# Second attention: an unread 128-row matmul ahead of each natural score pair

## The chip, the cores and the metric

One Trainium2 chip, one NeuronCore of it. The metric is the device time of one execution in microseconds, the median of several runs. TensorE's clock is granted by the chip at one of two levels, 2.4 GHz (shown as 1.00 or 9 in the profile) and 1.2 GHz (0.50 or 5).

## What is computed

Two blocks, each a gated attention and a gated feed-forward part on 2048 tokens of width 128. The part that matters here is the attention of the second block, after a layer norm. x has the shape (1, 2048, 128), so all 2048 tokens attend to each other, in 16 heads of width 8:

```python
qkv = (jnp.einsum('bnd,ed->bne', x, qkv_w) + qkv_b).reshape(b, n, H, 3 * HD)
q, k, v = jnp.split(qkv, 3, axis=-1)
attn = jax.nn.softmax(jnp.einsum('bhqd,bhkd->bhqk', q, k) * SCALE, axis=-1)
out = jnp.einsum('bhqk,bhkd->bhqd', attn, v)
out = out.transpose(0, 2, 1, 3).reshape(b, n, d)
return jnp.einsum('bnd,ed->bne', out, fc_w) + fc_b + x
```

In front of it stand a spectral attention with convolutions and a three-layer feed-forward part; behind it a mixture of eight experts of which two are chosen for each token.

## The kernel before, in words

Each engine runs a program of its own, written out by hand in order, with semaphores between them. The second attention is the part of TensorE's program between L738 and the end of the steps.

Layout. The 16 heads are four head groups (hg) of four heads (g). A head has 8 dimensions, and its queries and keys are stacked so that they take 32 rows of the array: head g of a group lies in rows 32g to 32g+31 of `Ks` and `Qb` (single-pass fp32r). Four matmuls that use the four different strips can run side by side.

Two kinds of scores are computed. *Natural* scores (`nat`, L768) have queries on the output partitions; VectorE takes their maximum per query (L1215). A natural item k has four matmuls of 32 rows by 512 columns into PSUM banks 0 to 3, as two pairs: pair 0 is heads 0 and 1, pair 1 is heads 2 and 3. Each pair waits until VectorE has reduced what the two banks held (`nat_max`, L765) and signals `nat_ready`. *Transposed* scores (`scores(g)`, L828) have keys on the output partitions, and take the negated maximum in as two more rows of `Qb`; they go to three rotating banks (4, 5, 7), ScalarE takes the exponential (L484), and `values` (L806) multiplies by V into bank 6: 128 rows by 16 columns, one column strip for each head, in two passes, eight records.

Order. A query block qb has 512 queries and there are four; a step s is one head group and one block of 128 keys (kt = s % 16), so 64 steps a query block, 256 in all, in groups of 16. The natural items run 20 steps ahead (`LEAD`). A step on TensorE is

```python
scores(0); nat(qb, s - 1 + LEAD, 1); scores(1); values(qb, s - 1)
scores(2); nat(qb, s + LEAD, 0); scores(3)
```

with the transposes of the maxima (`max_rows`, L780) after it in step kt = 13 and those of the finished outputs (`turn_outputs`, L794) in step kt = 2. A group's first step waits for the maxima to be in `Qb` (`mrow_in`): VectorE copies them (L1241), and SyncE writes them with eight transfers (L277). Steps 4 to 67 of a query block are a hardware loop run three times; the first four steps and the last sixty are written out. Natural items end 20 steps before the last step.

Ahead of the steps stands an opening loop of 16 natural items (32 pairs) between the projections (`stack`, L742: 128 rows by 512 columns, two-pass fp32) and the value tiles (L751), and then four natural items by themselves. Behind the steps come the output projection and the experts (`three`, L676 to L678: 128 rows by 512 columns in single-pass fp32r; `down`, L935; a transpose of 8 rows, L955).

Of the kernel before, what the change touches and what calls it, by code (L numbers as in the profile page):

```python
# [19 lines left out]
P = 128  # L20
# [49 lines left out]
def adaln_pair(nc, x_in, consts_in, mods_in, spectral_in, ffn_in, attn_in, moe_in, out):  # L70
    with ExitStack() as ctx:
        def sb(name, shape, dt=F32, where=ctx):
            return where.enter_context(nc.sbuf_tensor(name, shape, dt))
# [78 lines left out]
        with l1:  # L152
            Ks = sb("Ks", [P, HG, TOK], F32R, where=l1)
# [49 lines left out]
        def bank(n):  # L203
            return ps[:, n, :]
# [8 lines left out]
        def due(count):  # L213

            return not isinstance(count, int) or count > 0
# [29 lines left out]
        def between(slot):  # L245

            total = len(stacks) - early + NT // 2
            lo, hi_ = early + total * slot // 32, early + total * (slot + 1) // 32
            n = len(stacks)
            return range(min(lo, n), min(hi_, n)), range(max(lo, n) - n, max(hi_, n) - n)  # L250
# [305 lines left out]
        def _(pe):  # L556
# [3 lines left out]
            for layer in range(2):  # L560
                for k in range(6):
                    last = pe.matmul(ps[:, 7, 6 * layer + k:6 * layer + k + 1],
                                     dw_[f"wmod{layer}"][:, k * P:k * P + P], silu[:, layer:layer + 1],
                                     start=True, stop=True)
            last.then_inc(sem.mod_ready, 1)

            for u in range(8):
# [3 lines left out]
                for i in range(2):  # L571
                    last = pe.matmul(ps[:, u % 4, i * 4 * M:(i + 1) * 4 * M], z[:, 2 * u + i, :], dw_["dft"],
                                     start=True, stop=True)
# [6 lines left out]
            for n in range(4):  # L580
                for i in range(2):
                    b = 2 * n + i
                    last = pe.matmul(ps[:, 4 + n, 256 * i:256 * i + 256], sw["qw"][:, b * P:b * P + P], low_flat,
                                     start=True, stop=True)
                last.then_inc(sem.qkv_ready, 1)
            for j in range(2):
                last = pe.matmul(ps[:, 0, 256 * j:256 * j + 256], sw["kw"][:, j * P:j * P + P], low_flat,
                                 start=True, stop=True)
            last.then_inc(sem.qkv_ready, 1)
            for ri in range(2):  # L590
                last = pe.matmul(ps[:, 1, 256 * ri:256 * ri + 256], low_flat[:, ri * P:ri * P + P], sw["vw"],
                                 start=True, stop=True)
# [24 lines left out]
            for i, (ri, j) in enumerate(groups):  # L617
# [6 lines left out]
                if i + 4 < len(groups):  # L624
# [4 lines left out]
                          start=True, stop=True).then_inc(sem.o_ready, 1)  # L629
# [6 lines left out]
            for ri in range(2):  # L636
                pe.wait_ge(sem.gelu_ready, ri + 1)
                for half in range(2):
# [3 lines left out]
                              start=True, stop=True).then_inc(sem.pw_ready, 1)  # L642
# [8 lines left out]
            for b in range(4):  # L651
                pe.wait_ge(sem.yT_copied, b + 1)
                pe.matmul(bank((5 + b) % 8), dw_["idft"], YT[:, 4 * b:4 * b + 4, :].rearrange("p t d -> p (t d)"),
                          start=True, stop=True).then_inc(sem.idft_ready, 1)
# [83 lines left out]
            def stack(n):  # L738
                kq, hg, tb = stacks[n]
                if due(n - 3):  # L740
                    pe.wait_ge(sem.kq_done, n - 3)
                pe.matmul(bank(4 + n % 4), aw[("kw1", "qw1")[kq]][:, hg * P:hg * P + P],  # L742
                          hT[:, tb * 512:tb * 512 + 512], start=True, stop=True).then_inc(sem.kq_ready, 1)

            def value_tiles(u):
                pe.wait_ge(sem.kq_done, min(len(stacks), len(stacks) - 3 + u))
                if due(u - 3):
                    pe.wait_ge(sem.v_copied, u - 3)
                for i in range(2):
                    t = 2 * u + i  # L750
                    last = pe.matmul(ps[:, 4 + u % 4, 256 * i:256 * i + 256], hT[:, t * P:t * P + P], aw["vw1"],  # L751
                                     start=True, stop=True)
                last.then_inc(sem.v_ready, 1)

            def nat(qb, k, pair):

                hg, qt, c = k // 16 % 4, k % 16 // 4, k % 4
                item = 64 * qb + k
                if pair == 0 and k % 16 == 0:
                    if isinstance(qb, int) and qb == 0 and k == 0:  # L760
                        pe.wait_ge(sem.first_filled, 1)
                    else:
                        pe.wait_ge(sem.q_filled, 4 * qb + k // 16)
                if due(2 * item + pair - 1):
                    pe.wait_ge(sem.nat_max, 2 * item + pair - 1)  # L765
                for g in (2 * pair, 2 * pair + 1):
                    rows = slice(32 * g, 32 * g + 32)
                    last = pe.matmul(bank(g), Qb[rows, hg, qt * P:qt * P + P], Ks[rows, hg, c * 512:c * 512 + 512],  # L768
                                     start=True, stop=True)
                last.then_inc(sem.nat_ready, 1)  # L770
# [39 lines left out]
            def step(qb, s):  # L810
# [21 lines left out]
                if not first and not (last_block and s - 1 + LEAD >= 64):  # L832
                    nat(qb, s - 1 + LEAD, 1)
# [4 lines left out]
                if not (last_block and s + LEAD >= 64):  # L838
                    nat(qb, s + LEAD, 0)
# [8 lines left out]
            pe.wait_ge(sem.kq_done, early)  # L848
            for k in range(16):
                for half in range(2):  # L850
                    nat(0, k, half)
                    some_stacks, some_values = between(2 * k + half)
                    for n in some_stacks:
                        stack(n)
                    for u in some_values:
                        value_tiles(u)
# [621 lines left out]
```

## Time and profile before

| | us |
|---|---|
| Median of 3 runs | 1482.05 |
| Lowest, highest | 1471.12, 1508.8 |
| The profiled execution, its own time | 1492.91 |
| Span of its profile (first to last instruction) | 1491.1 |
| Mean granted TensorE clock in it | 0.842 |

PE is the matmul side of TensorE, PEld its weight loads, DVE VectorE, ACT ScalarE, POOL GpSimd, SPq the queue of SyncE. L828 is line 828 of the kernel. Matmul records overlap and their ends are modelled, so starts are the sounder thing to compare. Times in the profile's views are microseconds from the start of the span.

### The profile page before, as it was taken

Reading aid. Unit: us, or ns where it says so; the run is one execution under the profiler, and the core shown is the slowest. Engines: PE = TensorE matmul, PEld = TensorE weight load, DVE = VectorE, ACT = ScalarE, POOL = GpSimd, SP = SyncE. Lnnn points to the kernel's source line nnn. Section 1 sums busy time; section 2 is a strip of 40 time slices with the busy share of each in tenths; the row PEclk is TensorE's granted clock in tenths of the full one; section 3 lists DMA queues with packets and bytes.
Section 4 is the critical chain, followed back from the end, with each engine's and each line's share of the span. In section 5 each row is a group of like instructions: output and inputs, shape, how many; then the busy total and the mean of one; then the engine's idle time right before and its main releaser. Section 6 shows DMA issues by size and latency. Waiting matters only on the chain.

```text
span 1491.1 us, 19855 instructions
## 1 busy us (share of the span) xinstructions
PE 1271.4 (85%) x6846; PEld 620.4 (42%) x6846; DVE 874.1 (59%) x1244; ACT 796.4 (53%) x1423; POOL 18.0 (1%) x25
## 2 busy tenths in 40 slices
PE   4767999887988888888879988988898869999998
PEld 4435787332232222223322222322222127787877
DVE  4756442797687786778866578777870052122122
ACT  3335442433576676667755567666775554344442
POOL 0010000000000000000000000000000000000000
PEclk9868999795598897889975579878985579999999
DMA  8000000000000000000000000000000000000000
GB/s 330 1 1 0 0 0 1 0 0 1 1 1 2 1 2 3 1 2 1 1 3 1 1 1 2 1 2 1 2 1 1 0 0 1 7 1 7 0 7 7
DMA packets 9279, 14.82 MB, mean 10 GB/s; under 512 B 4320, under 2 KB 8544, under 8 KB 8672
## 3 DMA queue, kind: packets, MB, share of 16 engines
q1 hardware_dynamic: 8896, 10.84, 2.0%
q10 hardware_dynamic: 288, 2.76, 0.4%
q8 instruction: 53, 0.87, 0.2%
q14 instruction: 42, 0.34, 0.1%
HBM read 12.29 MB, written 1.05 MB: 9 GB/s over the span
## 4 chain that ended last, share of the span: by engine, by line
PE 65%; DVE 13%; ACT 11%; SPq 4%; issue 4%; DMA 2%; DVEq 0%; ACTq 0%
PE ps L806 19%; PE ps L828 17%; PE ps L935 8%; ACT probs L484 7%; DVE mx L1215 5%; PE ps L676 5%; PE ps L678 4%; PE ps L677 4%; SPq L277 4%; DMA Qb<-mT 2%; ACT eh L536 1%; PE ps L713 1%; PE ps L916 1%; PE ps L742 1%; PE ps L794 1%
## 5 line engine op out<-in xcount | busy, mean ns | idle before, releaser
L1215 DVE TENSOR_REDUCE mx<-ps 128x2 f32<-128x1024 f32 x512 | 605.6, 1218 | 183.0 <-PE ps L768 179.7
L484 ACT ACTIVATE probs<-ps 128x512 f32<-128x512 f32 x1024 | 534.3, 599 | 321.3 <-PE ps L828 319.7
L828 PE MATMUL ps<-Qb,Ks 32*128 32x512 f32 x1024 | 368.4, 574 | 111.8 <-ACT probs L484 71.9
L828 PEld LDWEIGHTS ps<-Qb,Ks 32*128 32x128 f32 x1024 | 145.9, 219 | 510.4 <-ACT probs L484 347.3
L806 PE MATMUL ps<-probs,V 128*16 128x512 f32 x2048 | 353.3, 756 | 0.0
L768 PE MATMUL ps<-Ks,Qb 32*128 32x512 f32 x1024 | 260.5, 561 | 14.3 <-DVE mx L1215 8.4
L536 ACT ACTIVATE eh<-ps,MW 128x512 f32<-128x512 f32 x128 | 87.9, 688 | 95.3 <-PE ps L678 94.6
L768 PEld LDWEIGHTS ps<-Ks,Qb 32*128 32x128 f32 x1024 | 105.7, 216 | 53.3 <-DVE mx L1215 35.2
L935 PEld LDWEIGHTS ps<-MW,eh 128*128 128x128 f32 x1024 | 118.3, 192 | 2.6
L935 PE MATMUL ps<-MW,eh 128*128 128x128 f32 x1024 | 119.2, 275 | 0.0
L1358 DVE SCALAR_TENSOR_TENSOR acc<-ps,gate,acc 128x128 f32<-128x128 f32 x128 | 36.0, 344 | 129.3 <-PE ps L935 128.8
L806 PEld LDWEIGHTS ps<-probs,V 128*16 128x16 f32 x2048 | 40.8, 98 | 80.2 <-ACT probs L484 52.5
L676 PE MATMUL ps<-hT,ew 128*128 (+1 forms) x128 | 56.7, 443 | 2.8
L678 PE MATMUL ps<-hT,ew 128*128 (+1 forms) x128 | 50.4, 394 | 0.0
L677 PE MATMUL ps<-hT,ew 128*128 (+1 forms) x128 | 50.3, 393 | 0.0
L1248 DVE RECIPROCAL rden<-ps 128x16 f32<-128x16 f32 x16 | 4.0, 248 | 76.5 <-PE ps L794 76.5
L1170 DVE TENSOR_TENSOR act_b<-bf,act_b 128x512 fp32r<-128x512 f32 x16 | 11.1, 692 | 58.9 <-ACT bf L435 58.9
L742 PE MATMUL ps<-hT,AW 128*128 128x512 f32 x64 | 38.9, 709 | 0.9 <-ACT hT L337 0.9
L676 PEld LDWEIGHTS ps<-hT,ew 128*128 128x128 f32 x128 | 24.0, 188 | 26.6 <-ACT eh L536 21.5
L676 PE MATMUL ps<-act_a,h 128*128 128x512 f32 x64 | 25.2, 394 | 1.6 <-DVE act_a L1147 1.6
L678 PEld LDWEIGHTS ps<-hT,ew 128*128 128x128 f32 x128 | 24.1, 188 | 5.7
L666 PE MATMUL ps<-CW,z 128*128 128x128 f32 x48 | 12.4, 430 | 16.4 <-DVE z L987 16.4
(214 smaller groups left out, 1026.9 us busy)
## 6 DMA issues: line engine op xcount, KB each, us to landing
MW<-moe_in SPq DMA_DIRECT2D x1, 4454.0 KB, 23.8
FW<-ffn_in SPq DMA_DIRECT2D x1, 2824.5 KB, 12.4
Qb<-mT SPq DMA_DIRECT2D x128, 2.0 KB, 1.7
SW<-spectral_in ACTq DMA_DIRECT2D x1, 1479.5 KB, 9.6
DW<-mods_in ACTq DMA_DIRECT2D x1, 1219.0 KB, 6.2
x<-x_in SPq DMA_DIRECT2D x4, 256.0 KB, 10.7
out<-x SPq DMA_DIRECT2D x4, 256.0 KB, 2.3
AW<-attn_in SPq DMA_DIRECT2D x1, 836.5 KB, 13.9
```

The lines of the kernel that those rows point to most:

```text
L277: sp.dma_start(Qb[row:row + 1, hg, :].bitcast(F32), mT[4 * part + g:4 * part + g + 1, :].bitcast(F32)) \
L484: act.activation(probs[:, 4 * (s % 2) + g, :], bank(score_bank[4 * (s % 16) + g]), ACT.Exp, scale=SCALE1) \
L536: act.activation(eh[:, e % 2, fb, :], bank(fb % 2), ACT.Relu, bias=mw["eb1"][:, col:col + 1]).then_inc(sem.eh_copied, 1)
L676: pe.matmul(to, w[0], v[0], start=start, stop=False)
L677: pe.matmul(to, w[0], v[1], start=False, stop=False)
L678: return pe.matmul(to, w[1], v[0], start=False, stop=stop)
L742: pe.matmul(bank(4 + n % 4), aw[("kw1", "qw1")[kq]][:, hg * P:hg * P + P], hT[:, tb * 512:tb * 512 + 512], start=True, stop=True).then_inc ...
L768: last = pe.matmul(bank(g), Qb[rows, hg, qt * P:qt * P + P], Ks[rows, hg, c * 512:c * 512 + 512], start=True, stop=True)
L806: last = pe.matmul(ps[32 * g:32 * g + VW, 6, :], V[:, kt, col:col + VW], probs[:, 4 * (s % 2) + g, :], start=(kt == 0), stop=(kt == 15))
L828: pe.matmul(bank(score_bank[n]), Ks[rows, hg, kt * P:kt * P + P], Qb[rows, hg, :], start=True, stop=True).then_inc(sem.st_ready, 1)
L935: last = pe.matmul(ps[:, 2 + e % 2, qt * P:qt * P + P], eh[:, e % 2, fb, qt * P:qt * P + P], mw["ew2"][:, col:col + P], start=(fb == 0), s ...
L1215: dve.tensor_reduce(mx[:, k // 16 % 2, k % 16 // 4, k % 4, 2 * pair:2 * pair + 2], ps[:, 2 * pair:2 * pair + 2, :], AX, ALU.max) \
```

## The change

`nat` gets a parameter, true except in the opening loop of 16 items. Where it is true, a matmul of 128 rows by 512 columns in fp32r (weights: the first 128 columns of the head group's `Ks`; moving: the 512 columns of the pair's keys) is issued into the first bank of the pair, after the pair's wait and ahead of its two matmuls. It starts and stops its own accumulation, and the pair's first matmul overwrites the bank.

```diff
-            def nat(qb, k, pair):
+            def nat(qb, k, pair, filled=True):
...
                 if due(2 * item + pair - 1):
                     pe.wait_ge(sem.nat_max, 2 * item + pair - 1)
+                if filled:
+                    pe.matmul(bank(2 * pair), Ks[:, hg, 0:P], Ks[:, hg, c * 512:c * 512 + 512], start=True, stop=True)
                 for g in (2 * pair, 2 * pair + 1):
...
             for k in range(16):
                 for half in range(2):
-                    nat(0, k, half)
+                    nat(0, k, half, False)
```

## Rows read from the trace of the kernel before

**Rows 1.** The page: busy time of each engine, and TensorE's granted clock in 40 slices

```profile
PE 1271.4 (85%) x6846; PEld 620.4 (42%) x6846; DVE 874.1 (59%) x1244; ACT 796.4 (53%) x1423; POOL 18.0 (1%) x25
...
PEclk9868999795598897889975579878985579999999
```

**Rows 2.** Stretches: length; PE, PEld, DVE, ACT, POOL busy (count); clock, DMA share, GB/s

```profile
349.40:408.60 59.20, 54.80 (x234) 14.18 (x237) 35.77 (x34) 30.18 (x58) 0.00 (x0) 0.50 0.00 1
408.60:459.80 51.20, 41.66 (x296) 14.57 (x292) 43.89 (x43) 37.91 (x73) 1.23 (x2) 1.00 0.01 2
770.40:862.60 92.20, 84.32 (x363) 21.47 (x363) 53.17 (x51) 45.85 (x88) 0.61 (x1) 0.50 0.01 1
...
1122.00:1200.50 78.50, 65.53 (x232) 14.65 (x232) 1.23 (x3) 39.59 (x77) 0.00 (x0) 0.50 0.00 1
```

**Rows 3.** Timeline, full clock: start, duration, engine, line, [idle before <-releaser]

```profile
696.13 0.72 PE L828 MATMUL ps<-Qb,Ks 32*128 32x512 f32 x2
...
696.65 2.06 ACT L484 ACTIVATE probs<-ps 128x512 f32<-128x512 f32 x4 [0.57 <-PE ps L828]
...
697.30 0.50 PE L828 MATMUL ps<-Qb,Ks 32*128 32x512 f32 x1 [0.33 <-ACT probs L484]
...
697.73 1.09 PE L806 MATMUL ps<-probs,V 128*16 128x512 f32 x8
...
698.76 0.72 PE L828 MATMUL ps<-Qb,Ks 32*128 32x512 f32 x2
```

**Rows 4.** Timeline, a step at half clock

```profile
841.23 0.79 PE L828 MATMUL ps<-Qb,Ks 32*128 32x512 f32 x1
...
841.83 0.62 PE L828 MATMUL ps<-Qb,Ks 32*128 32x512 f32 x1
...
842.71 0.79 PE L828 MATMUL ps<-Qb,Ks 32*128 32x512 f32 x1 [0.25 <-ACT probs L484]
...
843.43 1.91 PE L806 MATMUL ps<-probs,V 128*16 128x512 f32 x8
845.26 0.28 PEld L828 LDWEIGHTS ps<-Qb,Ks 32*128 32x128 f32 x1 [1.69 <-issue]
```

**Rows 5.** Timeline, opening loop at full clock: natural pair, projection, natural pair

```profile
286.11 0.50 PE L768 MATMUL ps<-Ks,Qb 32*128 32x512 f32 x2
...
286.54 0.30 PEld L742 LDWEIGHTS ps<-hT,AW 128*128 128x128 f32 x2 [0.25 <-issue]
...
287.60 0.18 PEld L768 LDWEIGHTS ps<-Ks,Qb 32*128 32x128 f32 x2 [0.76 <-issue]
```

**Rows 6.** Timeline, experts: 128-row matmuls in a row, both clocks; then 8 rows

```profile
1258.28 0.40 PE L677 MATMUL ps<-hT,ew 128*128 128x512 f32 x1
1258.51 0.40 PE L678 MATMUL ps<-hT,ew 128*128 128x512 f32 x1
...
1230.83 0.63 PE L678 MATMUL ps<-hT,rw 128*128 128x512 f32 x1
1231.26 0.63 PE L676 MATMUL ps<-hT,rw 128*128 128x512 f32 x1
...
1252.96 0.39 PE L678 MATMUL ps<-hT,ew 128*128 128x512 f32 x1
1253.28 0.96 PEld L955 LDWEIGHTS ps<-MW,gtT 8*128 8x128 f32 x8 [0.35 <-issue]
```

**Rows 7.** Timeline: transposes of outputs (half clock) and maxima, and a group's first score

```profile
833.41 1.11 PE L794 MATMUL ps<-CW,U 128*128 128x128 f32 x4
...
834.45 0.79 PE L828 MATMUL ps<-Qb,Ks 32*128 32x512 f32 x1
...
652.41 0.60 PE L780 MATMUL ps<-CW,m 128*8 128x128 f32 x4 [0.58 <-ACT probs L484]
...
652.94 0.49 PE L828 MATMUL ps<-Qb,Ks 32*128 32x512 f32 x1
...
660.42 0.49 PE L828 MATMUL ps<-Qb,Ks 32*128 32x512 f32 x1 [2.94 <-DMA Qb<-mT]
```

## The prediction

> **What bounds the kernel now.** I read the page first. TensorE is busy for 85% of the span, the other engines for at most 59%, and the row of the granted clock is uneven between the tenth and the thirty-third of the forty slices, which is the second attention [rows 1]. So the second view is the table of stretches, cut where the clock changes [rows 2]. At full clock (1.00, which is 2.4 GHz) the stretch 408.6 to 459.8 us runs 73 exponentials, that is 18.3 steps at four per step, or 2.80 us a step with all group ends in it. At half clock (0.50, 1.2 GHz) the stretch 770.4 to 862.6 runs 88, that is 22 steps at 4.19 us. The attention ends at 1200.5, and of its 850 us the half clock holds 59, 92 and 78 us in three long stretches [rows 2], the rest in short dips. In both states TensorE's records cover over 80% of the stretch.
>
> The third view is the timeline of single steps. At full clock [rows 3] a step repeats every 2.63 us (696.13 to 698.76): a cluster of scores and natural pairs, whose small matmuls use different 32-row strips and run side by side; 0.52 us after its start the first of four exponentials begins; the score at 697.30 waits 0.33 us for an exponential to free its bank; the values of the step before start at 697.73, when the last exponential that they need is done, and take 1.02 us. TensorE is the longest part of that loop but has a gap in it. At half clock [rows 4] the same loop takes 4.03 us (841.23 to 845.27); values take 1.84 us of it.
>
> **The change, part by part.** It adds to each natural pair, except the 32 of the opening loop, one 128-row weight load and one matmul of 512 columns. Natural pairs number 512 (two for each of 256 items), so 480 fillers: 8 before the steps, 472 in steps 0 to 236 of 256. The last 20 steps have no natural pairs and get none. No wait is added: the wait on the row maximum, already there, now stands ahead of the filler. No transfer, no VectorE, ScalarE or GpSimd work is added. Nobody reads the filler, but TensorE takes its matmuls in order, so everything behind it is later.
>
> What does one cost? The trace has it in two forms. Between matmuls of its own kind (128 rows, 512 columns, single pass) starts are 0.23 us apart at full clock and 0.43 at half, the next weights loading underneath [rows 6]. But the filler stands between 32-row matmuls. Where the trace changes the rows used, the next weight load doesn't start until the matmul ahead has run out: from a natural pair at 286.11 to the load of a 128-row matmul at 286.54 are 0.43 us [rows 5], and from a 128-row matmul at 1252.96 to an 8-row load at 1253.28 are 0.32 us without a load of its own [rows 6]; with the load, about 0.11 more, that is again 0.43. From the 128-row matmul the natural pair follows only after it has run out too, at 287.60 [rows 5]. At half clock the same block is 0.72 us (score at 842.71 to values at 843.43 [rows 4]). Bounds for a filler: 0.23 to 0.43 us at full, 0.43 to 0.72 at half. Below nothing is possible only through the clock, and is treated with the rivals. I take the upper ends, because they are the rows with a change of rows in them, in both directions.
>
> The filler also cuts the clusters. The order of a step is score 2, filler, natural pair 0, score 3, score 0 of the next step, filler, natural pair 1, score 1, values. Score 2 now stands alone: one block. Natural pair 0 with score 3 is a block, and score 0 shares rows with the pair, so it follows as a second wave: at full clock that costs 0.22 more (0.72 against 0.50 us for one [rows 3]), at half 0.43 more (841.83 + 0.62 against 841.23 + 0.79 [rows 4]). Natural pair 1 with score 1 is one block. A step is then:
> full clock: 4 x 0.43 (score 2, two fillers, pair 1 with score 1) + 0.65 + values 1.02 = 3.39 us, against 2.63;
> half clock: 4 x 0.72 + 1.15 + 1.84 = 5.87 us, against 4.03.
> The gaps in which TensorE waited for exponentials (0.33 us at full clock) are used up in this; four exponentials (2.06 us [rows 3]) and two maxima fit inside either step, so neither ScalarE nor VectorE is late next. TensorE has no gap left.
>
> **Which clock.** This decides. Before the steps the clock is at half from 340, with VectorE setting the pace of the natural pairs; fillers fill part of those gaps but leave others, so I expect the steps to begin at half clock as now. Does the filler lift it? In the old half-clock step the columns stream, weighted by the share of the array's rows in use, for 1.71 us in the values (four passes at 0.43 [rows 6]) and 0.43 x (1 + 0.75 + 0.25) in the scores and pairs: 2.56 of 4.03 us, 64%. In the new one it is 1.71 + 0.43 x (0.25 + 1 + 0.75 + 0.25 + 1 + 0.75) = 3.42 of 5.87 us, 58%. So a step gets no denser: running out and reloading eat what the filler adds. The old, denser step stayed at 0.50 from 349.4 to 408.6 and from 770.4 to 862.6 [rows 2]. So I take it that the new one stays at half clock through the filled steps. At full clock the share is 1.71 of 3.39, 50%, beside 1.28 of 2.63, 49%, which held; the full clock would hold too, once reached.
>
> The Trainium skill, "TensorE: Matmul & The Clock Gate", section "Why this matters for your kernels", says the opposite: keep TensorE continuously busy and it comes to the full clock. By that rule the filled steps run at 3.39 us and the time is that of the second rival. The trace doesn't bear it out: TensorE's records cover 84.32 of 92.2 us at 0.50 [rows 2].
>
> **The sum.** Steps start at 352 (349.4 now [rows 2], and some 2.6 for eight fillers). 236 filled steps x 5.87 = 1385. In 14 groups the output transposes (833.41 to 834.45, 1.04 us at half) and the maximum transposes (652.41 to 652.94, 0.53 at full [rows 7], say 0.8 at half) also cut the second wave off its first, 0.29 each: 14 x 2.42 = 34. The stall at a group's start goes: from the maximum transposes at 652.41 to the score at 660.42 that waits for the transfers are 8.0 us [rows 7], and two steps of 5.87 cover that. Last 20 steps at half clock as now: 78.5 us for 77 exponentials [rows 2], 4.08 a step, 82. End of the attention 1853. The tail is unchanged: 1491.1 - 1200.5 = 290.6, and 1.8 lies outside the span (1492.9 less 1491.1). 1853 + 290.6 + 1.8 = 2145 us. The profiled execution is 11 us above the median of the runs shown; where the clock is pinned that luck falls away, so I correct nothing. If the clock does this, 2090 to 2180.
>
> **Rivals.**
> Late escape: the half clock is left somewhere and kept for a part. For it: at 862.6 the old kernel got out of a long stretch with no change of pattern [rows 2], and the shares above are near each other. Against it: 58% is under 64%. Halfway between this forecast and the next rival, 1850.
> Full clock from the first steps: 352 + 236 x 3.39 (800) + 14 x 1.95 (27: transposes 0.6 and 0.53, 0.22 for each cut, and 0.4 of stall, since two steps of 3.39 cover nearly all of the 8.0) + 82 + 290.6 + 1.8 = 1553. Against it: the steps start at half clock, see above. Still slower.
> Not slower: the fillers' loads hide under the matmul ahead. Mechanism: the pitch of 0.23 us [rows 6] holds in the clusters too; two fillers then add 0.46 us where 0.33 to 0.6 of gap is; a full-clock step stays near 2.7 us, and at half clock the share that streams rises to 3.42 in about 4.6 us, 74%, so that the clock comes up soon. 352 + 236 x 2.7 (637) + 14 x 5 for group ends + 82 + 292 = 1433. It decides as soon as a filler costs under about 0.3 us at full clock. Against it stand the 0.43 us of [rows 5]; for it, that the 128-row matmul there is a two-pass one.
> The Trainium skill, same page, section "Part 2: What happens when you issue a matmul", has this rule: a weight load is pulled ahead of running matmuls when it goes to the background weight buffer. By it the time is this rival's; the 0.23 us pitch agrees, the 0.43 us across a change of rows doesn't.
>
> **Numbers.** Half clock throughout 0.50, late escape 0.22, full clock 0.14, hidden 0.12, the rest for what I don't see. The range 1540 to 2180 takes in the first three. A measurement of this kernel tells about 2% from no change: 1452 to 1512. The hidden case lies two thirds under that and one third in it. Faster 0.08, same 0.05, slower 0.87.
>
> **What would show it.** Right: a line of its own with 480 matmuls; a filler's load 0.4 us (full) or 0.7 us (half) behind the score ahead; steps of 5.9 or 3.4 us with no idle ahead of L828 from ScalarE; ScalarE waiting longer for scores; granted clock 0.50 from 350 to about 1850; no transfer wait at group starts. Wrong: filler loads starting within 0.15 us of the matmul ahead, or a clock row at full height in the attention.

## The result, and the profile after

The changed kernel takes 2165.62 us (median of 4 runs, 2160.24 to 2168.71); the kernel before, run beside it, 1495.42 (1471.12 to 1512.06). The ratio is 1.466, 95% interval 1.456 to 1.477. Ratios are of the fast runs of each kernel alone; in the experiments below that leaves out two of the four runs of the kernel with strips, one of which took 1860 us.

The page of the changed kernel: the engines, TensorE's granted clock in 40 slices, and two of the costliest groups (busy us, mean ns | idle before, and what ended it). The filler is L767, the natural matmuls L770, the scores L830, the values L808.

```profile
PE 2043.8 (95%) x7326; PEld 852.4 (39%) x7326; DVE 896.0 (42%) x1244; ACT 846.4 (39%) x1423; POOL 18.0 (1%) x25
...
PEclk9789995555555555555555555555555555699999
...
L484 ACT ACTIVATE probs<-ps 128x512 f32<-128x512 f32 x1024 | 584.3, 596 | 935.4 <-PE ps L830 934.0
...
L767 PE MATMUL ps<-Ks 128*128 128x512 f32 x480 | 381.7, 795 | 2.3 <-DVE V L1211 2.2
```

The clock row that was uneven [rows 1] is now flat at half through the whole second attention. 480 fillers are there. ScalarE does the same 1024 exponentials and now waits 934 us for scores: TensorE has become the bound of every filled step. The stretches show the same (length, busy time of PE, PEld, DVE, ACT, POOL, clock): the filled steps, the last twenty, the tail.

```profile
343.99:1781.72 1437.73, 1427.44 (x4353) 441.15 (x4352) 603.13 (x570) 550.14 (x957) 7.36 (x12) 0.50 0.00 1
1781.72:1868.60 86.88, 72.80 (x265) 16.65 (x262) 4.47 (x9) 44.06 (x84) 0.00 (x0) 0.51 0.00 1
1868.60:2158.40 289.80, 268.27 (x1636) 211.19 (x1634) 79.68 (x261) 122.11 (x184) 0.00 (x0) 0.98 0.01 4
```

TensorE's records cover 1427 of 1438 us, and the clock is 0.50 all along. The 290.6 us behind the attention are 289.8 now, so all of the loss lies in it: 851 us (349.4 to 1200.5 [rows 2]) have become 1525.

The timeline of one filled step, beside [rows 4]:

```profile
899.97 0.79 PE L770 MATMUL ps<-Ks,Qb 32*128 32x512 f32 x2
...
901.12 0.80 PE L767 MATMUL ps<-Ks 128*128 128x512 f32 x1
...
901.84 0.28 PEld L770 LDWEIGHTS ps<-Ks,Qb 32*128 32x128 f32 x2 [0.44 <-issue]
...
902.57 1.91 PE L808 MATMUL ps<-probs,V 128*16 128x512 f32 x8
...
904.41 0.28 PEld L830 LDWEIGHTS ps<-Qb,Ks 32*128 32x128 f32 x1 [1.69 <-issue]
...
905.13 0.80 PE L767 MATMUL ps<-Ks 128*128 128x512 f32 x1
...
905.86 0.79 PE L770 MATMUL ps<-Ks,Qb 32*128 32x512 f32 x2
```

From 899.97 to 905.86 are 5.89 us. Read the starts: two waves of pair 0, score 3 and score 0 take 1.15, the filler 0.72, pair 1 with score 1 0.73, the values 1.84, score 2 alone 0.72, and the second filler 0.73 before pair 0 again. The weight loads wait 0.44 us with "issue" as the cause: nothing that the profile shows holds them. I read these waits as the matmul ahead running out of the array; the runs below bear on that.

### The profile page after: what moved, and what is told of

It reads as the page before. It is cut to its first block, busy times and chain, and to the rows that moved or that the text cites. A ratio compares the mean times of both kernels' runs of the same rounds, so it can differ in the third digit from the quotient of the medians.

```text
span 2158.4 us, 20815 instructions
## 1 busy us (share of the span) xinstructions
PE 2043.8 (95%) x7326; PEld 852.4 (39%) x7326; DVE 896.0 (42%) x1244; ACT 846.4 (39%) x1423; POOL 18.0 (1%) x25
## 4 chain that ended last, share of the span: by engine, by line
PE 90%; DVE 5%; ACT 3%; issue 1%; DMA 1%; SPq 0%; DVEq 0%; ACTq 0%
PE ps L808 22%; PE ps L770 16%; PE ps L767 16%; PE ps L830 15%; PE ps L937 5%; PE ps L676 3%; PE ps L678 3%; PE ps L677 3%; DVE mx L1217 1%; ACT eh L536 1%; ACT probs L484 1%; PE ps L796 1%; PE ps L782 1%; PE ps L713 1%; PE ps L918 1%; PE ps L742 1%
## 5 line engine op out<-in xcount | busy, mean ns | idle before, releaser
L1217 DVE TENSOR_REDUCE mx<-ps 128x2 f32<-128x1024 f32 x512 | 627.2, 1225 | 834.2 <-PE ps L770 834.0
L484 ACT ACTIVATE probs<-ps 128x512 f32<-128x512 f32 x1024 | 584.3, 596 | 935.4 <-PE ps L830 934.0
L830 PE MATMUL ps<-Qb,Ks 32*128 32x512 f32 x1024 | 706.2, 759 | 22.9 <-ACT probs L484 22.9
L808 PE MATMUL ps<-probs,V 128*16 128x512 f32 x2048 | 489.1, 1048 | 0.0
L830 PEld LDWEIGHTS ps<-Qb,Ks 32*128 32x128 f32 x1024 | 264.3, 292 | 481.2 <-issue 427.5
L770 PE MATMUL ps<-Ks,Qb 32*128 32x512 f32 x1024 | 396.2, 772 | 7.8 <-DVE mx L1217 5.2
L767 PE MATMUL ps<-Ks 128*128 128x512 f32 x480 | 381.7, 795 | 2.3 <-DVE V L1211 2.2
L770 PEld LDWEIGHTS ps<-Ks,Qb 32*128 32x128 f32 x1024 | 142.6, 276 | 242.8 <-issue 215.7
L767 PEld LDWEIGHTS ps<-Ks 128*128 128x128 f32 x480 | 138.2, 288 | 253.2 <-issue 229.6
L808 PEld LDWEIGHTS ps<-probs,V 128*16 128x16 f32 x2048 | 38.1, 107 | 113.0 <-issue 105.5
L676 PEld LDWEIGHTS ps<-hT,ew 128*128 128x128 f32 x128 | 24.0, 188 | 26.6 <-ACT eh L536 20.6
```

The costliest lines, as they stand in the source:

```text
L484: act.activation(probs[:, 4 * (s % 2) + g, :], bank(score_bank[4 * (s % 16) + g]), ACT.Exp, scale=SCALE1) \
L676: pe.matmul(to, w[0], v[0], start=start, stop=False)
L767: pe.matmul(bank(2 * pair), Ks[:, hg, 0:P], Ks[:, hg, c * 512:c * 512 + 512], start=True, stop=True)
L808: last = pe.matmul(ps[32 * g:32 * g + VW, 6, :], V[:, kt, col:col + VW], probs[:, 4 * (s % 2) + g, :], start=(kt == 0), stop=(kt == 15))
L830: pe.matmul(bank(score_bank[n]), Ks[rows, hg, kt * P:kt * P + P], Qb[rows, hg, :], start=True, stop=True).then_inc(sem.st_ready, 1)
L1217: dve.tensor_reduce(mx[:, k // 16 % 2, k % 16 // 4, k % 4, 2 * pair:2 * pair + 2], ps[:, 2 * pair:2 * pair + 2, :], AX, ALU.max) \
```

## The experiments

Each says on which kernel it is built; the first four are the changed kernel with the edit shown. Where one run is given, there was one.

**The filler on one 32-row strip.** Is it the columns, or the change of the array's shape?

```diff
-                    pe.matmul(bank(2 * pair), Ks[:, hg, 0:P], Ks[:, hg, c * 512:c * 512 + 512], start=True, stop=True)
+                    own = slice(64 * pair, 64 * pair + 32)
+                    pe.matmul(bank(2 * pair), Ks[own, hg, 0:P], Ks[own, hg, c * 512:c * 512 + 512], start=True, stop=True)
```

> The filler keeps its 512 columns and its place, but uses only the 32-row strip of the pair's first matmul, so no change of the rows in use stands in the cluster. Theory (a change of rows makes the next weight load wait until the matmul ahead has run out): the fillers form waves of 0.43 us at half and 0.22 us at full clock beside the others, four waves a step, and end before the exponentials that the values wait for; a step keeps its 4.0 us at half and 2.63 us at full clock, the columns stream for a larger part of it (2.9 of 4.0 us, weighted by rows, against 2.56 of 4.03), and the clock is at full for most of the attention: 1420 to 1500 us. Rival (the price is that of 480 more matmuls of 512 columns in TensorE's order, whatever their rows): as the change, 2050 to 2170 us.

Measured: 1468.42 us (median of 4), ratio to the kernel before 0.979 (0.968 to 0.991). The same 480 matmuls of 512 columns in the same places, on a quarter of the rows, cost nothing in a plain step: it takes 2.63 us at full clock and 4.04 at half, beside 2.63 and 4.03. Steps with transposes do get longer (of the outputs 5.18 for 4.52 us at half clock, of the maxima 3.39 for 3.17 at full). The time lies in the theory's range, and the rival falls. The timeline at full clock:

```profile
424.95 0.49 PE L768 MATMUL ps<-Ks 32*128 32x512 f32 x1
...
425.51 0.49 PE L768 MATMUL ps<-Ks 32*128 32x512 f32 x1
...
427.58 0.49 PE L768 MATMUL ps<-Ks 32*128 32x512 f32 x1
```

So the price is neither that of 480 more matmuls nor that of their columns wherever they stand. The 1860 us of one run has no trace, but its mean granted clock is on record, 0.549 beside 0.872 to 0.899 in the other three: the half clock held there for most of the kernel, with the same instructions.

**The filler with 128 columns.** How much of a block is columns?

```diff
-                    pe.matmul(bank(2 * pair), Ks[:, hg, 0:P], Ks[:, hg, c * 512:c * 512 + 512], start=True, stop=True)
+                    pe.matmul(ps[:, 2 * pair, 0:P], Ks[:, hg, 0:P], Ks[:, hg, c * 512:c * 512 + P], start=True, stop=True)
```

> The filler keeps its 128 rows but moves 128 columns in place of 512. Theory (run-out and reload at each change of rows, plus the columns): each filler costs 0.32 us less at half clock, a step 5.25 us in place of 5.89, the clock stays at half, 236 x 0.64 less than the change: 2010 us. Rival (the price is the columns): the filler shrinks to 0.11 us, the step to 4.2 us, 1530 to 1600 us.

Measured: 2008.18 us (one run). The timeline gives the step, 699.93 to 705.17, 5.24 us, and the filler's block, 700.65 to 701.05, 0.40 in place of 0.72:

```profile
699.93 0.79 PE L830 MATMUL ps<-Qb,Ks 32*128 32x512 f32 x1
700.65 0.48 PE L767 MATMUL ps<-Ks 128*128 128x128 f32 x1
701.05 0.79 PE L770 MATMUL ps<-Ks,Qb 32*128 32x512 f32 x2
...
705.17 0.79 PE L830 MATMUL ps<-Qb,Ks 32*128 32x512 f32 x1
```

The theory had 5.25 us and 2010 us; the rival falls. A quarter of the columns takes off 0.32 of 0.72 us. At that rate the 128 columns left are 0.11 us, and the other 0.29 of the 0.40 don't hang on the columns: I read them as load and run-out.

**The filler ahead of pair 1 only.**

```diff
-                if filled:
+                if filled and pair == 1:
```

> The filler stands ahead of pair 1 only, so score 2, pair 0 and score 3 are one cluster again. Theory: a half-clock step is 1.15 + 0.72 + 0.72 + 1.84 = 4.43 us; if the clock stays at half, 1820 us; weighted by rows the columns stream for 2.99 of 4.43 us, 67%, between the old step (64%) and what I can't see, so it may also come up, and then a step is near 2.65 us and the time 1450 to 1500. Rival (each filler costs half of the change's 1.86 us a step): 4.96 us a step, 1945 us.

Measured: 1543.38 us (one run). The half-clock step is 4.44 us (354.38 to 358.82), the full-clock step 2.64 (375.89 to 378.53). In each group but the last, most of which has no fillers, the clock is up again after up to ten half-clock steps, and the mean granted clock is 0.846:

```profile
354.38 1.91 PE L808 MATMUL ps<-probs,V 128*16 128x512 f32 x8
...
358.82 1.91 PE L808 MATMUL ps<-probs,V 128*16 128x512 f32 x8
```

```profile
375.89 1.10 PE L808 MATMUL ps<-probs,V 128*16 128x512 f32 x8
...
378.53 1.09 PE L808 MATMUL ps<-probs,V 128*16 128x512 f32 x8
```

The block arithmetic holds to 0.01 us, and the rival (4.96 us a step) falls. Half the fillers cost 60 us (beside 1482.99 for the kernel before), not half of 670: taking one away shortened the step by 1.45 us, and it also let the clock come up. The total lies between the two outcomes that were named.

**The clock lifted by other means.** Three further 128-row matmuls behind the values in the second step of each group, the change otherwise as it is.

```diff
+            def behind(qb, s):
...
+                if kt == 1:
+                    if ended:
+                        pe.wait_ge(sem.nat_max, 8 * 64)
+                    else:
+                        pe.wait_ge(sem.nat_max, 2 * (64 * qb + s + LEAD) - 1)
+                    for _ in range(3):
+                        pe.matmul(bank(0), Ks[:, hg, 0:P], Ks[:, hg, 0:512], start=True, stop=True)
...
                     values(qb, s - 1)
+                    behind(qb, s)
```

> The change as it is, and in addition three 128-row matmuls of 512 columns right behind the values in the second step of each group (48 in all), where the rows in use are 128 already. Theory (the filled step holds whichever clock it finds): the dense stretch of values and three fillers lifts the clock to full, the filled steps then run at 3.4 us, a group near 56 us, and the time is 1560 to 1620 us. Rival (the filled step can't hold the full clock, or isn't lifted by so few): above 2000 us, with the clock up for a few steps of a group at most.

Measured: 1868.18 us (one run), neither theory's number. The stretches tell why:

```profile
333.00:746.00 413.00, 409.70 (x1234) 128.78 (x1234) 175.25 (x165) 152.72 (x266) 2.45 (x4) 0.50 0.00 1
841.00:893.00 52.00, 51.28 (x271) 18.17 (x270) 36.22 (x36) 33.75 (x59) 0.61 (x1) 0.99 0.01 1
902.00:954.00 52.00, 51.28 (x269) 18.19 (x267) 36.00 (x36) 33.34 (x58) 0.61 (x1) 0.99 0.01 1
963.00:1033.00 70.00, 67.42 (x352) 24.44 (x348) 46.28 (x46) 43.16 (x75) 0.61 (x1) 0.99 0.01 2
1033.00:1217.00 184.00, 182.55 (x554) 56.51 (x553) 75.46 (x71) 69.03 (x120) 1.23 (x2) 0.50 0.00 1
```

In the first four groups the extra matmuls don't lift it, in the fifth they do, in the tenth they don't again. Both later stretches at half clock, 756 to 842 and 1033 to 1217, begin at the turns of the hardware loop, behind waits of 2.10 and 1.86 us that nothing in the profile releases. Where the clock is up, filled steps hold it through a group at 3.36 us (forecast 3.39):

```profile
1246.78 1.05 PE L808 MATMUL ps<-probs,V 128*16 128x512 f32 x8
...
1250.14 0.62 PE L808 MATMUL ps<-probs,V 128*16 128x512 f32 x4
```

They don't hold it from group to group. At the starts of four groups (892.8, 954, 1268 and 1330 us) it falls behind a wait of 0.72 us for an exponential, with no wait for a transfer:

```profile
892.05 0.50 PE L841 MATMUL ps<-Qb,Ks 32*128 32x512 f32 x1 [0.72 <-ACT probs L484]
...
892.99 0.79 PE L770 MATMUL ps<-Ks,Qb 32*128 32x512 f32 x2
```

So half clock and filler are two prices. At full clock the two fillers cost 0.73 us a step, the half clock 2.53 more on top. And 48 further unread matmuls made the changed kernel 297 us faster, since they brought the clock up for part of it.

**One filler behind the values, built on the kernel before.** 128 rows follow 128 rows there.

```diff
+            def behind(qb, s):
...
+                if not ended:
...
+                        pe.wait_ge(sem.nat_max, 2 * (64 * qb + s + LEAD) - 1)
+                    for _ in range(1):
+                        pe.matmul(bank(0), Ks[:, hg, 0:P], Ks[:, hg, 0:512], start=True, stop=True)
...
                     values(qb, s - 1)
+                    behind(qb, s)
```

`ended` is true in the last steps, those without natural pairs. The trace has 235 of these fillers: the first step has no values.

> The kernel before, and in each step that has natural pairs one 128-row filler of 512 columns right behind the values (236 in all), where 128 rows are in use already; it is written to bank 0, which natural pair 0 of the same step overwrites. Theory (the run-out comes with a change of the rows in use, not of the columns): the filler follows the last matmul of the values without a run-out and adds 0.23 us to a full-clock step (2.86) and 0.43 to a half-clock step (4.46); its columns join the densest part of the step, so the long half-clock stretches go and a dip at a group's start ends in a few steps: 1430 to 1510 us. Rival (any 128-by-128 load waits for the run-out here too): 0.43 and 0.72 a step, 3.06 and 4.75, and 1520 us or more.

Measured: 1501.17 us (one run), beside 1485.38 for the kernel before. My theory as I had put it falls, the rival has the step, though the total is under its 1520: from the filler to the next matmul 0.43 us, and 3.06 and 4.76 us a step.

```profile
461.93 0.51 PE L819 MATMUL ps<-Ks 128*128 128x512 f32 x1
462.36 0.49 PE L839 MATMUL ps<-Qb,Ks 32*128 32x512 f32 x1
```

The values use 128 rows but strips of columns, so the shape changes here as well. The clock did gain (0.925 in this run against 0.833 to 0.883 in the thirteen of the kernel before), which pays for the fillers and no more.

**Fillers only where the clock has just fallen, built on the kernel before.** The filler of the last experiment, in three steps of a group.

```diff
-                if kt == 1:
+                if kt in (1, 2, 3):
...
-                    for _ in range(3):
+                    for _ in range(1):
```

The lines are set against those of the lifted kernel above.


> As the run before it, but with the filler behind the values in three steps of each group only, the second to the fourth, where the clock has just fallen (48 fillers). Theory (the stretches at half clock are what is worth removing, and a dense spot behind the values ends them): no half-clock stretch longer than 20 us in the attention, the last group included; 48 x 0.23 = 11 us are paid, and about 96 half-clock steps in the trace of before become about 45, 50 x 1.4 us: 1410 to 1450 us, 2 to 5% faster than before. Rival (fillers lift the clock only where they stand in the natural pairs' place, or not at all): 1480 to 1520 us.

Measured: 1496.67 us, ratio 1.014 (1.008 to 1.019): a miss. The rival's range has the total. In its trace half-clock stretches of 68, 44, 31 and 82 us are left; 48 blocks of 0.43 to 0.73 us are paid. In this place a filler doesn't pay for itself.

**No filler; the maxima earlier, built on the kernel before.** What drops the clock in the kernel before?

```diff
-LEAD = 20
+LEAD = 22
...
-        turn_kt, rows_kt = 2, 13
+        turn_kt, rows_kt = 2, 11
```

> The kernel before without any filler, but with the natural items 22 steps ahead in place of 20 and the maximum transposes in step 11 of a group in place of 13, so that the maxima are in Qb before the next group begins: from the transposes to the first score of the next group are then four full-clock steps and more, 10.5 us, against the 8.0 us that the copy and the transfers take. Theory (the clock falls in the wait of about 3 us at a group's start, and steps hold the level that they have): no wait for the transfers, once the clock is full it stays so from group to group; the first group still runs at half clock. 14 or 15 waits of 3 us and as many dips of some 5 us go: 1350 to 1400 us. Rival (the clock falls for another reason, the turn transposes or the thin last steps): the waits go, the dips stay, 1430 to 1450 us.

Measured: 1394.85 us, median of 4 runs (1372.14 to 1414.2), beside 1485.38 for the kernel before, in the theory's range. No score waits for the transfers any more ([rows 7] shows that wait, 2.94 us), and the clock is carried from group to group. The first group didn't stay at half clock, as I had expected: it left it after three steps. The edit does one thing more: it changes the order of the three banks, so that a group's first score no longer takes the bank of the score just ahead. The clock still falls in the last steps, which have no natural pairs (1021.6, with no wait over 0.7 us in the 12 us ahead), and at the two turns of the loop over the query blocks, where TensorE waits 2.7 and 3.1 us for nothing that the profile shows and goes on at half clock:

```profile
541.35 0.49 PE L828 MATMUL ps<-Qb,Ks 32*128 32x512 f32 x1
...
544.58 0.78 PE L828 MATMUL ps<-Qb,Ks 32*128 32x512 f32 x1 [2.72 <-issue]
```

**Both together, on the kernel before.** The three lines of the last diff and the fillers of the one ahead of it.

> Both together: natural items 22 steps ahead, and a 128-row filler behind the values in the second to the fourth step of each group. Theory: as the run before it, and the clock comes up within the first group too (12 half-clock steps less, 17 us), for 48 x 0.23 = 11 us of fillers: 1340 to 1390 us, and a smaller spread from run to run. Rival (once the waits are gone the fillers have nothing to lift): 11 us slower than the run before it.

Measured: 1399.1 us (median of 5, 1395.41 to 1416.4), ratio 0.940 (0.932 to 0.948). The theory fails: nothing is gained over the kernel without fillers, whose first group was up after three steps anyway. Whether it is 11 us slower, as the rival has it, can't be told: the medians are 4 us apart and the runs overlap.

**The loops written out, with and without the earlier maxima; and the earlier maxima with strip fillers.**

```diff
-            with pe.Fori(0, TB - 1) as qb:
+            for qb in range(TB - 1):
                 for s in range(4, 68):
                     step(qb, s)
```

and the same for ScalarE and VectorE. The kernel with strips keeps its loops; it is the changed kernel with the strip edit from above and the two lines of the earlier maxima.

> The kernel before with the natural items 22 steps ahead, and the hardware loops over the query blocks of the second attention written out on TensorE, ScalarE and VectorE. In the run with 22 steps ahead a step of 5.2 to 5.5 us stands where the loop turns over (541.35 to 544.57, nothing issued for 3.0 us and no engine waited for), and the half-clock stretches of 17 and 34 us begin there. Theory (any wait of some 3 us, whatever its cause, drops the clock): without the turn of the loop there is no such step and no such stretch: two waits of 2.5 us and two stretches (17 and 34 us, of which a third is loss, 17 us) go, 1360 to 1380 us. Rival (the written-out program waits for its own instructions elsewhere): as the run with the loop, 1370 to 1415 us, with waits that nothing releases scattered over the attention.

> Natural items 22 steps ahead, loops as before, and ahead of each natural pair a filler on the 32-row strip of the pair's first matmul (480 of them, 512 columns, as in the run with one strip). Theory (a filler in a strip of its own costs nothing where TensorE has a gap, and a step that streams more leaves the half clock sooner): full-clock steps stay 2.63 us, the half-clock stretches at the start and at the turns of the loop end within three steps; 1360 to 1390 us. Rival (fillers of 32 rows don't bring the clock up, or cost some 0.1 us a step): 1395 us or more.

> The kernel before with its loops over the query blocks written out, natural items 20 steps ahead as before. Theory: the waits for the transfers and their dips stay, the steps at the turns of the loop (5.11 and 5.33 us in the trace of before, the second of which begins the half-clock stretch of 92 us) go: 1430 to 1480 us. Rival (the turn of the loop costs nothing that shows in the total): as before, 1450 to 1505 us.

Measured: earlier maxima and loops written out 1373.19 us, ratio 0.926 (0.920 to 0.931), the lowest median here: 7% under the kernel before and 37% under the changed one, and in the theory's range. Its runs (1370.54 to 1379.62) overlap with those of the earlier maxima with loops (1372.14 to 1414.2), so how much the loops add there is open; the spread is smaller. With strips and loops 1381.1, ratio 0.929 (0.925 to 0.934), in the theory's range too: the half-clock stretches end after two, four and three steps, where the theory had three at most. Loops written out alone 1427.88 (one run, beside 1493.67), 2 us under the theory's range and outside the rival's. The turns aren't all of that gain. A group's first values start 4.4 us behind those ahead in most groups, where the kernel before has 4.6 to 6.0 in the looped ones but the first, and the first group leaves the half clock after three steps, where the trace of before has it for fifteen. The stretches of the first of the three: from its fifth step to the last ones the clock is 0.98, and no wait of TensorE in the attention is over 1.6 us.

```profile
368.00:1027.00 659.00, 580.81 (x3928) 200.78 (x3921) 570.60 (x567) 507.70 (x977) 7.39 (x12) 0.98 0.01 1
1027.00:1078.00 51.00, 43.28 (x151) 9.04 (x150) 0.00 (x0) 25.34 (x50) 0.00 (x0) 0.50 0.00 0
```

TensorE is busy for 88% of the first stretch at full clock; in the changed kernel it was 99% at half.

## Why the prediction was right or wrong

**What bounds, and the pinned clock: right, the reason not shown.** The filled steps run at 0.50 from the first to the last, no step of theirs escapes it, and the spread of the runs falls from 41 us to 8.5. The prediction got there by comparing how large a share of a step the columns stream. No run shows that this share decides: the same steps came up in the lifted kernel in one group and not in another, and one run of the kernel with strips stayed low where three came up.

**The price of a filler: right.** 0.72 us at half clock (0.72 measured), 0.43 at full (0.42 to 0.44 in the lifted kernel); step 5.87 forecast, 5.89 measured; 3.39 and 3.36. The second wave and score 2 alone came as worked out. The other rule of the Trainium skill that I should have weighed is in "TensorEngine Tiling (Array Packing)", section "Tiling Modes": changing the tiling mode, and not just the tile, drains TensorE. The trace agrees in all three places, 0.44 us of unexplained wait at half clock ahead of the filler's load, the pair's and that of the values, and the strip filler, which stays in the mode of 32 rows by 128 columns, pays nothing. My wording, a change of the rows in use, was too narrow: the values and a 128-by-128 filler use the same rows and the run-out is there (the filler behind the values). The rule of the page covers both.

**Full clock by being busy: rightly set aside.** 1427 of 1438 us busy at 0.50 speak against it, and so does the fastest kernel, less busy (581 of 659 us) and at 0.98.

**How thin a step is: right in order.** With a filler ahead of each pair, of 512 or of 128 columns, no filled step left the half clock. With one filler a step the clock came up in each group that had them, with the strip it mostly did within a few steps, and in the kernel before at times. That is the order in which the prediction had put the old and the new step; that this is what counts isn't proven by it. One more sign points that way: in the traces of the kernel before and of the earlier maxima the clock falls in the last steps (1122.0 and 1021.6), which have no natural pairs, and no wait there is over 0.8 us.

**The sum: 2145 forecast, 2165.6 measured. The step that failed is the term for the ends of the groups, 34 us where the trace has 51.** Against the 1482 us shown, 2145 is a ratio of 1.447, under the interval of 1.456 to 1.477. By the profiled execution (2160.2; the median is 5 us above it) the terms stand so:

| term | forecast | measured |
|---|---|---|
| first score | 352 | 344 |
| 236 filled steps without the ends of groups | 1385 | 1386 (5.89 each, the first one shorter) |
| ends of 14 groups | 34 (2.42 each) | 51 (3.67 each) |
| last 20 steps | 82 | 87 |
| behind the attention, outside the span | 292.4 | 291.6 |

So the mis-sized term is 17 us too small; the last 20 steps add 5. The output transposes cost 1.34 us (1.33 forecast) and the maximum transposes 1.24 (1.09), but a third place was missing, a wait that the prediction put at nothing: the first score of a group can't join the second wave. The order of the three banks starts anew there, so it takes the bank of the score just ahead (bank 4 both times) and waits for that one's exponential.

```profile
435.41 0.79 PE L830 MATMUL ps<-Qb,Ks 32*128 32x512 f32 x1
...
436.92 0.79 PE L830 MATMUL ps<-Qb,Ks 32*128 32x512 f32 x1 [0.72 <-ACT probs L484]
```

1.52 us between these two where the wave costs 0.43: 1.09 a group, 15 us in 14. The order of the banks stands in the kernel before as well, and I had looked there only at the wait for the transfers. The first score came 8 us early: the opening ended 6.4 us earlier in this execution (the first matmul behind the value tiles starts at 333.1, where it was 339.4), and the eight fillers filled gaps there and cost 0.9 us where 2.6 had been put. That early start is luck, and it masked a third of the error of 23 us in the other terms.

**The rivals.** Late escape (1850) and hidden loads (1433) didn't happen. The full clock (1553) didn't either, but the lifted kernel shows its steps. The prediction's sentence that the full clock would hold once reached is right inside a group only: in the lifted kernel it fell at the starts of four groups and at both turns of the loop, so a start at full clock would hardly have given 1553. The upper end 2180 was tight: the measured median lies 14 us under it, and 1.466 times the 1482 shown is 2173.

## What to carry to other kernels

Price a matmul put between others by whether it changes the shape in which the array is tiled: if so it costs its load, its columns and the running out on both sides, and splits the waves around it. To keep the clock up, look first for the waits behind which it falls and take them out (an earlier producer, a loop written out): that gave 6 to 7% here, and no filler gave that by itself. In the kernel before these waits are 2.1 to 3.7 us; with a filler behind each step's values the clock also fell behind two of 1.66 us, and with fillers in the pairs behind four of 0.72. Unread work where it splits the clusters makes a step longer and didn't bring the clock up; the same work behind the values brought it up in some groups and not in others.

## What I had not expected of the hardware

The hardware loop has 64 unrolled steps on three engines and turns twice. Wherever the clock was full ahead of a turn, TensorE waited 1.9 to 3.1 us there, nearly always with no releaser, and went to half clock soon after, which cost more than the wait: 17 and 34 us of half clock in the kernel with the earlier maxima, by its steps of 4.03 and 2.63 us about a third of it loss. In the changed kernel, at half clock, the turn costs nothing: the steps there take 5.89 us like all others. What TensorE waits for at a turn stays open.

And the clock isn't decided by the program alone. Three full-array matmuls right behind the values failed to lift it in five groups and did it in others with the same instructions. The kernel before and the one with its loops written out have the same first four steps, begun within 0.1 us of each other; one stayed at half clock until 408.6, the other was up at 364.1.
